# A vision block in four chunks: two chunks' steps woven together after each scan, the routing weights brought by DMA, the loop written out

## What is computed

```python
h = patches @ W.T + b                                   # 768 -> 192
x = layernorm(h); r = rmsnorm(x)
z = (r @ W_in.T) * sigmoid(r @ W_gate.T)                # 192 -> 384
dt_in, B, C = split(z @ W_xproj.T)                      # 96, 16, 16
dt = softplus(dt_in @ W_dt.T + b_dt)
state[t] = exp(dt*A)*state[t-1] + (dt*z)*B[t]           # 384 channels x 16 states
y = sum_n(state*C) + D_skip*z
x = x + y @ W_out.T
x = x + (silu(rms(x) @ W_g.T) * (rms(x) @ W_up.T)) @ W_down.T
h = h + x
t = rmsnorm(layernorm(h)) * scale                       # the mixture
w = softmax(top4(t @ gate_w.T + gate_b))                # a weight per token and expert
g, l = split(t @ w1[e] + b1[e])                         # for each of 16 experts
out = sum_e w[e] * ((min(g,7)*sigmoid(1.702*g)*(clip(l)+1)) @ w2[e] + b2[e])
h = h + layernorm(h) + out
```

## Time and profile before

| | |
|---|---|
| median of 3 runs | 804.27 us (803.79 to 808.25) |
| the profiled execution | 805.15 us, its span 803.4 us |
| busy in the span | PE 634.8 us, DVE 523.8, ACT 275.0, POOL 273.9 |
| mean granted TensorE clock | 0.881 of full speed |
| DMA | 65.97 MB, mean 82 GB/s |

### The profile page before, as it was taken

The page is one execution under the profiler, slowest core; times in us unless marked ns, Lnnn a source line. Parts: engine busy times, 40 slices in busy tenths (PEclk is TensorE's granted clock), DMA queues, the critical chain, the costliest instruction groups (busy, mean ns, idle before and its releaser), DMA issues.

```text
span 803.4 us, 10289 instructions
## 1 busy us (share of the span) xinstructions
PE 634.8 (79%) x2853; PEld 465.5 (58%) x2853; DVE 523.8 (65%) x1104; ACT 275.0 (34%) x623; POOL 273.9 (34%) x266
## 2 busy tenths in 40 slices
PE   5766566698676889978768788988778788976996
PEld 4443344577554657757545556757655456755774
DVE  4268892246699785545689895555579896555664
ACT  1285451023734322213734231203644341212331
POOL 2437793012244541212145452122135453112322
PEclk8768897889689899979779999979869899987999
DMA  6934351413011011122111011122110110221430
GB/s 202 295 138 140 122 192 59 176 45 110 17 53 60 1 60 60 63 82 89 59 59 59 0 59 59 59 71 103 60 59 1 59 59 18 100 71 59 155 141 11
DMA packets 15153, 65.97 MB, mean 82 GB/s; under 512 B 2464, under 2 KB 7888, under 8 KB 9808
## 3 DMA queue, kind: packets, MB, share of 16 engines
q1 hardware_dynamic: 15104, 65.47, 23.8%
HBM read 55.12 MB, written 10.32 MB: 81 GB/s over the span
## 4 chain that ended last, share of the span: by engine, by line
PE 47%; DVE 27%; issue 11%; ACT 9%; POOL 4%; DVEq 1%; DMA 0%; ACTq 0%; POOLq 0%; SPq 0%
PE pa L488 27%; PE pb L488 20%; DVE state L983 9%; DVE pa L974 4%; DVE dt L959 4%; ACT scratch L751 3%; ACT a_bar L751 3%; POOL scratch L1224 2%; DVE hid L1129 2%; POOL root L1167 2%; ACT ffn L751 1%; DVE scratch L1120 1%; DVE scratch L1112 1%; DVE scratch L1104 1%; ACT c_all L751 1%
## 5 line engine op out<-in xcount | busy, mean ns | idle before, releaser
L488 PE MATMUL pa<-bc_parts,pick_state 128*128 128x288 f32 x256 | 109.4, 469 | 93.8 <-DVE state L983 78.7
L1212 POOL TENSOR_TENSOR read<-state,c_all 128x576 f32<-128x576 f32 x92 | 130.0, 1415 | 155.9 <-DVE state L983 149.9
L1224 POOL TENSOR_TENSOR scratch<-scratch 128x288 f32<-128x288 f32 x96 | 77.1, 803 | 266.0 <-DVE scratch L1120 266.0
L488 PE MATMUL pb<-t_high,w 128*128 128x288 f32 x576 | 156.0, 336 | 4.0 <-DVE scratch L1104 3.9
L983 DVE TENSOR_TENSOR_SCAN state<-a_bar,pa 128x288 f32<-128x288 f32 x192 | 144.3, 751 | 16.0 <-ACT a_bar L751 0.5
L488 PEld LDWEIGHTS pa<-bc_parts,pick_state 128*128 128x128 f32 x256 | 57.1, 226 | 143.4 <-DVE state L983 118.2
L751 ACT ACTIVATE a_bar<-dt,decay 128x280 f32<-128x280 f32 x192 | 97.6, 524 | 111.7 <-DVE state L983 111.7
L488 PE MATMUL pa<-read,ident 128*128 128x288 f32 x384 | 123.1, 449 | 6.0 <-DVE read L991 5.8
L751 ACT ACTIVATE scratch<-pb,vec 128x288 f32<-128x288 f32 x96 | 47.9, 499 | 204.2 <-PE pb L488 204.2
L488 PEld LDWEIGHTS pb<-t_high,w 128*128 128x128 f32 x576 | 106.4, 199 | 19.0 <-DVE scratch L1104 6.1
L488 PE MATMUL pb<-hid,w 128*64 128x288 f32 (+1 forms) x384 | 103.8, 462 | 11.5 <-DVE hid L1129 11.4
(11 more groups left out here) (132 smaller groups left out, 741.7 us busy)
## 6 DMA issues: line engine op xcount, KB each, us to landing
w<-w_store SPq DMA_DIRECT2D x32, 1152.0 KB, 5.1
w_store<-w SPq DMA_DIRECT2D x8, 1152.0 KB, 5.0
scratch<-expert_w SPq DMA_DIRECT2D x16, 384.0 KB, 5.6
x_patch<-patches SPq DMA_DIRECT2D x4, 864.0 KB, 4.6
w<-expert_w SPq DMA_DIRECT2D x1, 2304.0 KB, 9.9
x_patch<-patches SPq DMA_DIRECT2D x3, 288.0 KB, 4.1
w_embed<-embed_w SPq DMA_DIRECT2D x3, 256.0 KB, 3.8
hid<-unit_pick SPq DMA_DIRECT2D x1, 576.0 KB, 14.8
```

The source lines that it names most:

```text
L488: return nc.tensor.matmul(out, lhsT, rhs, start=start, stop=stop)
L1212: pool.tensor_tensor(read[:, i % READ_SLOTS, :], state[:, i % STATE_SLOTS, :], c_pair(i), ALU.mult)\
L1224: pool.tensor_tensor(glu, g_act, l_clip[un % 2], ALU.mult).then_inc(glu_ready.sem, 1)
```

## The change

After each scan, the post steps of chunk c and the pre steps of chunk c+1 are put in one list (`woven`), post on banks 0 and 1 of `pa`, pre on 2 and 3. Tiles that both need are doubled (`h0s`, `y1s`, roots, diagonals, semaphores) or laid elsewhere (`squares2` in `y`, `centered3` in `ffn`, `factors` apart from `ffn`). For chunks from 1 on, the log1p steps of the blocks 1 and 2 stand in pre and not in the scan. Of the pieces of B 39 stand in the scan (routing and 18 units) and 13 in the woven part (6 units). In the scan three banks take the fills, the fill of half g+2 stands behind the advance of g, and the decays come one step earlier. The bank for the routing weight and its products are gone; ACT writes half the weights to `mix_half`, SP stores them in DRAM and loads each unit's rows, spread over 64 partitions twice, in four slots of `route_rows`; the multiplication by them (scale) is POOL's. The loop over chunks is written out.

```diff
 def after_first(chunk):
-    return not isinstance(chunk, int)
+    return chunk > 0
...
+    def scan(c):
+        steps = [("decay", 0), ("fill", 0), ("fill", 1)]
+        for g in range(HALVES):
...
+            if k == 0 and i + 1 < SCAN_STEPS:
+                steps.append(("decay", i + 1))
+            steps.append(("advance", g))
+            if g + 2 < HALVES:
+                steps.append(("fill", g + 2))
+            if k:
+                steps.append(("read", i))
+                if i >= 2:
+                    steps.append(("collect", i - 2))
...
+    def woven(c):
+        before = pre(c + 1) if c + 1 < CHUNKS else []
+        after, mixed = list(post), []
+        for s in before:
+            for t in NEXT_PRE.get(s, ()):
+                while after and t in after:
+                    mixed.append((c, after.pop(0)))
+            mixed.append((c + 1, s))
+        return mixed + [(c, t) for t in after]
...
+PIECES_BEFORE = {("decay", 0): 1, ("advance", 4): 1, ("advance", 6): 1,
+                 **{("advance", 8 + n): 1 for n in range(36)}}
...
         def run(engine, steps):
-            for phase, step, i in ORDER:
-                if phase == "A" and step in steps:
-                    steps[step](0, i)
-                elif phase == "prologue" and step in steps:
-                    steps[step](i)
-            with engine.Fori(1, CHUNKS) as c:
...
+            for phase, c, step, i in ORDER:
+                name = "experts_" + step if phase == "B" else step
+                if name in steps:
+                    steps[name](c, i)
...
+            def load_route(un):
+                pair, k = divmod(un, 3)
+                slot = un % ROUTE_SLOTS
+                for half in range(2):
+                    e = 2 * pair + (k if k < 2 else half)
+                    sp.dma_start(route_rows[half * REST:(half + 1) * REST, slot, :],
+                                 mix_rows[e:e + 1, :].to_broadcast([REST, T])).then_inc(route_in[slot].sem, 16)
+
+            def experts_start(c, _):
+                sp.wait_ge(mix_halved.sem, mix_halved.at(c, 1))
+                sp.dma_start(mix_rows, mix_half[:, :]).then_inc(mix_kept.sem, 16)
+                sp.wait_ge(mix_kept.sem, mix_kept.at(c, 1))
+                for un in range(ROUTE_SLOTS):
+                    load_route(un)
+
+            def experts_scale(c, un):
+                if un + ROUTE_SLOTS < UNITS:
+                    sp.wait_ge(hid_ready.sem, hid_ready.at(c, un + 1))
+                    load_route(un + ROUTE_SLOTS)
...
+                elif g < 2:
+                    pe.wait_ge(bc_low.sem, bc_low.at(c, 1))
+                    if after_first(c):
+                        pe.wait_ge(base_ready.sem, base_ready.at(c - 1, 1))
+                        pe.wait_ge(t_ready.sem, t_ready.at(c - 1, 2))
                 else:
-                    pe.wait_ge(scanned.sem, scanned.at(c, g - 1))
-                spread(g % 2, 0, g % STATES).then_inc(pe_b.sem, 1)
+                    pe.wait_ge(scanned.sem, scanned.at(c, g - FILL_BANKS + 1))
+                spread(g % FILL_BANKS, 0, g % STATES).then_inc(pe_b.sem, 1)
...
-            def experts_scale(c, un):      # PE: the routing weight's product
-                if un:
-                    pe.wait_ge(hid_ready.sem, hid_ready.at(c, un))
-                mm(pb[:, WEIGHT, 0:T], pick_unit[:, un, :], mix_parts[:, :], True, True).then_inc(pe_weight.sem, 1)
...
-            def experts_scale(c, un):      # DVE
-                dve.wait_ge(glu_ready.sem, glu_ready.at(c, un + 1))
-                dve.wait_ge(pe_weight.sem, pe_weight.at(c, un + 1))
-                dve.tensor_tensor(hid[:, un % HID_TILES, :], glu, pb[:, WEIGHT, 0:T], ALU.mult)\
-                    .then_inc(hid_ready.sem, 1)
...
+            def experts_scale(c, un):      # POOL
+                pool.wait_ge(glu_ready.sem, glu_ready.at(c, un + 1))
+                slot = un % ROUTE_SLOTS
+                pool.wait_ge(route_in[slot].sem, route_in[slot].at(c, un // ROUTE_SLOTS + 1))
+                if un >= HID_TILES:
+                    pool.wait_ge(pe_hid.sem, pe_hid.at(c, (un - HID_TILES) // 2 + 1))
+                pool.tensor_tensor(hid[:, un % HID_TILES, :], glu, route_rows[:, slot, :], ALU.mult)\
+                    .then_inc(hid_ready.sem, 1)
```

More of the change, by code:

```diff
@@ L117, in schedule @@
-    for s in pre + scan + post:
-        last = s == ("scale3", 0)
-        for _ in range(min(len(pieces), len(pieces) if last else PIECES_BEFORE.get(s, 0))):
+    def woven(c):
[7 more added lines that the diff above has]
+        return mixed + [(c, t) for t in after]
@@ new lines, in schedule @@
+    stages.append(emit(0, [(0, s) for s in pre(0)], {}, {}))
+    for c in range(CHUNKS):
+        if c:
+            pieces, scaled, downs = experts(), -1, 0
+        last = c == CHUNKS - 1
+        stages.append(emit(c, [(c, s) for s in scan(c)], PIECES_BEFORE, DOWNS_BEFORE))
+        stages.append(emit(c, woven(c), PIECES_LAST if last else PIECES_WOVEN, DOWNS_LAST if last else DOWNS_WOVEN))
+    assert not halves
+    out = []
+    pieces, scaled, downs = experts(), -1, 0
+    while pieces:
+        issue(out, CHUNKS - 1, 1, 0)
+        issue(out, CHUNKS - 1, 1, 2)
@@ L159, in vit_tower @@
               identity, out_main, out_rest):
-    ORDER = schedule()
+    ORDER = [entry for stage in schedule() for entry in stage]
     with ExitStack() as ctx:
```

446 lines of the change are left out of this document (233 added, 213 removed).

## The result

The changed kernel takes 795.9 us (median of four runs, 793.4 to 797.3), the kernel before 806.3 in the same comparison: a ratio of 0.987, 95% interval 0.984 to 0.989. It is 1.3% faster, 10 us, where I had forecast 61. The profiled execution took 793.4 us (span 791.3) against 805.15 (803.4). In experiments 3 and 7 one execution each ran at a much lower granted clock (863 us at 0.68, 824 us at 0.76); the ratios leave these two out, and the medians given are 0.8 and 0.3 us higher for them.

What follows compares the result with a forecast made beforehand. DVE bounds the scans, PE with serial-chain waits bounds post and pre. Stage terms +2-7-25.5-27+0-3-1 sum to -61.5 from 805.15 us, giving 743 us on the median; range 700 to 780.

Steps and rivals of the forecast that it cites:

- Last experts: Expert units after the last post: a pair of units about 5.4 us, twelve pairs 65, stage -1 us from 82.
- Woven part without units: Between first scan and second: post and pre overlap, 91 us falls to 65.5, -25.5.
- The piece of 13.5 behind t_in: End of each woven part: t_in, base, t_low, two log1p, routing, decays and fills in series, 13.5 us with waits.
- Woven parts with units: The two later woven parts, six units each: 98 us falls to 84.5, -13.5 each, -27 together.
- Head: Before the first scan: two banks make two later inproj wait 0.9 us each, +2 us.
- First scan: Scan without units, 72 us: fills for a later half make a half 1.0 us; counted as -7 us.
- Last post: Post steps after the last scan, 48 us: six units instead of eight, two banks, -3 us.
- Scans: Three scans with 18 units: DVE with its waits sets steps of 3.7 us, 87 against 88, counted 0.
- rival A: Scans: POOL and DVE take turns, steps of 4.3 us, small gain, 770 us; chance 0.20.
- B: Large gain: clip falls in POOL's pauses, scan step 3.2 us, woven factor 1.15, 705 us; chance 0.14.
- C: Slower: routing rows come late by DMA and units wait; at 18 us per row 829 us; chance 0.07.
- D: No change: the weave does nothing, 91 and 98 us stay, scans cost the gain, 800 to 806; chance 0.03.

Runs made afterwards that it cites:

- experiment 3: Changed kernel with, on TensorE alone, a unit's gate products ahead of the fill that waits for VectorE's advance in the scans: 781.9 us, ratio 0.967 to the kernel before.
- experiment 7: Changed kernel with the sixteen copies of C as sixteen steps between squares and logarithms, all logarithms ahead of the third root's spread: 785.1 us.
- experiment 1: Changed kernel with the last stage's down products two units later in the order: 761.4 us, ratio 0.943 to the kernel before.
- experiment 10: Changed kernel with eleven useless 32-bit products on TensorE ahead of three waits of the first woven part: 791.9 us.
- experiment 8: Changed kernel with, on ScalarE alone, the square for the second variance ahead of the activations for the next chunk's h0: 796.0 us.
- experiment 9: Changed kernel with the second variance's square first on ScalarE and the first woven part's three weight splits moved into the first scan: 798.1 us.
- experiment 5: Changed kernel with a third PSUM bank for the copies of C in all four chunks: 789.5 us.
- experiment 4: Changed kernel with the steps between first scan and second chunk not woven, first all of post, then all of pre: 813.6 us.
- experiment 2: Changed kernel with the product that makes hid back on VectorE, routing rows still by DMA: 807.6 us.
- experiment 11: Changed kernel with two slots for the routing rows in place of four: 793.5 us.

## Why the prediction was wrong, step by step

*Last experts, "-1": the step that failed.* The term is "About 5.4 times 12 is 65", and the mistake in it is that "downs start with the first pair and not behind the ninth unit" was priced at nothing. I took the 5.5 us per pair of the earlier trace rows with its waits of 0.17 and 0.51, and changed the durations in it, but not the distance between a hid and the down that waits for it. A pair measured 7.8 us as a mean, twelve of them 94 and not 65. In the old order the down came 2.3 us of TensorE's work behind the linear half that its hid starts from; now it comes 0.66 behind it, and the chain from that half to hid (ScalarE's copy, clip, mix, glu, hid) takes 3.2. Experiment 1 shows it whole: with the downs two units later a pair takes 5.25 and the stage 82.0, against 81 of the forecast, and 30.5 us of the 50 that the traces miss are back (34.5 in the medians). GpSimd's hid and the rows from DRAM were priced rightly here: the forecast for the stage comes true with both in place.

*Woven part without units, 65.5 forecast, 76.3 measured.* The sum took TensorE's 37 us at full clock and added waits counted in the old part. The part has 50.9 us of TensorE at a clock of 0.81 (6.9 of it the sixteen spreads of C, which the 37 left out); the sum priced the work at one clock and took the waits from a part that had run at another. Experiment 10 shows 2.8 us of the 10.8 as clock, experiments 8 and 9 at most 1 to 3 as engine orders. The copies on two banks cost nothing here (experiment 5). Experiment 4 gives the weave itself as 16.7; I had counted on more of pre's 18 us of work falling into post's waits than do. Which waits of the rest, 5 to 7 us, are whose, no run separates. The piece of 13.5 behind t_in was right to 0.1 in every part.

*Woven parts with units: 84.5 forecast, 87.4 and 88.4 measured.* The factor of 1.25 taken from a stretch of the same kind came within 4 us, while the sum from prices at full clock was 11 off. The copies on two banks make 2.2 and 3.0 of these parts (experiment 5).

*Head, +2 forecast, +6.3 measured.* The later inproj were counted, the copies of C not: sixteen copies took 5.93 without a gap in the earlier trace rows, and on two banks a pair of 0.71 has a pause of 0.40 behind it, 8.4 for sixteen. That puts 2.2 on the path (9.1 from the first copy to the advance, where the kernel before and experiment 5 have 6.9). The three inproj rounds, counted as 1.8, took 3.4 more than before here and 1.6 more in six of the eleven traces with this code. The difference is the clock: in this trace the products of the second round run at a granted 0.50 (31 to 34 us), in experiment 1's at 1.00.

*First scan, -7: right* (-7.8 measured, a half in 1.01). *Last post, -3: right in sign,* -6.5.

*Scans, 87 forecast and 87.3, 88.7 and 87.2 measured, for a wrong reason; that the number came out is luck.* I had VectorE wait with the clip for GpSimd; it waited at the gate's bound for TensorE, which had waited for VectorE's advance. Experiment 2 shows the loop by what an addition costs (nearly all of it), experiment 3 by what breaking it gives. The contention of rival A was real but asleep.

*The rivals.* A's price did not fall due, B's step of 3.2 was not reached even by the best version (3.55 as a mean), and C is out (rows in 2.7 us, experiment 11). D's stages did not come either: the changes in the woven parts and the first scan are 43 us, and one place took 30 of them back.

## What to carry to other kernels

When a change moves a consumer nearer to its producer in an order, count the distance in the consumer's engine time against the length of the chain between the two, for each place where the order has a different rhythm: the same code with a lag in one stage and without one in another has two prices. When two engines both show small waits for each other in a loop, neither wait need be free room: here 0.45 us added to one came out nearly whole in each step. Reorder the one instruction group that the other stands for, and look for what the wait had been hiding. A stage's sum in full-clock prices wants a comparable stretch of the same trace beside it.

## What the runs showed of the hardware

The waits of the last stage were paid again in the clock: with the same instructions it needed 71.5 us of TensorE at 0.84 and 64.2 at 0.92 (experiment 1). Useless products in three waits brought the first 29 us behind the first scan from 0.75 to 1.00 and were worth 2.8 us (experiment 10). The clip, one SBUF input and no PSUM, took 0.30 to 0.31 us alone and 0.72 as a mean of eighteen when most fell beside a GpSimd product (experiment 3); the mix, with two SBUF inputs, took 0.46 alone and up to 1.10 when it started inside one (experiment 1). The clip ended 0.16 behind GpSimd's product and the mix 0.31. The advance and the fill, with an operand in PSUM, kept their 0.74 and 0.43 beside GpSimd's products. A DMA that spreads one row of DRAM over 64 partitions landed in 2.7 us as a median of 192.
